# One table phase per sample on ScalarE in the first attention, with two full products ahead of each set of score tiles

## The reference, cut to what matters

```python
x = x + _L0_attn_a_ref(_layernorm(x), Wq, Wk, Wv, Wo)
x = x + _L0_ffn_ref(_layernorm(x), router_w, e_bias, Wg, Wu, Wd, SWg, SWu, SWd)
x = x + _L0_attn_b_ref(_layernorm(x), qkv_w, qkv_b, proj_w, proj_b)
x = x + _L0_ffn_ref(_layernorm(x), router_w, e_bias, Wg, Wu, Wd, SWg, SWu, SWd)

# _L0_attn_a_ref, 16 heads of 8 features
diff_sq = jnp.maximum(q_norm_sq + k_norm_sq - 2.0 * qk, 0.0)
denom = jnp.maximum((1.0 - q_norm_sq) * (1.0 - k_norm_sq), 1e-06)
cosh_arg = jnp.maximum(1.0 + 2.0 * diff_sq / denom, 1.0)
distance = jnp.where(cosh_arg > 1.0, jnp.arccosh(jnp.maximum(cosh_arg, 1.0 + 1e-12)), 0.0)
attn = jax.nn.softmax(-distance, axis=-1)

# _L0_ffn_ref routes each token: sigmoid scores, the best 4 of 8 groups by their two best
# experts, the best 8 experts in them, and their scores normalised are the coefficients
```

## Time and profile before

| | |
|---|---|
| time, median of 3 runs | 1120.06 us (1116.53 to 1122.86) |
| the profiled execution | 1117.54 us, its span 1115.8 us |
| PE, DVE, ACT, POOL busy | 88%, 88%, 62%, 32% of the span |
| mean granted TensorE clock | 0.86 of full speed |

### The profile page before, as it was taken

How to read it: one execution, slowest core, us unless ns; L and a number is a source line. 1 busy time by engine, 2 the same in 40 slices (tenths; PEclk the granted TensorE clock), 3 DMA queues, 4 the chain that set the end, 5 groups by cost and what they waited for, 6 DMA issues and landing times. The chain is left out here.

```text
span 1115.8 us, 17424 instructions
## 1 busy us (share of the span) xinstructions
PE 976.6 (88%) x5387; PEld 705.7 (63%) x5387; DVE 977.7 (88%) x1480; ACT 693.2 (62%) x791; POOL 359.8 (32%) x226
## 2 busy tenths in 40 slices
PE   7756766676768999999999899999879999999997
PEld 5533434343437788888888645455557888888886
DVE  7799888988978999999999787889688999999997
ACT  4789999999965445554455553666635445554454
POOL 2045655565450334333332120100112333433330
PEclk9855555555558999999999998999989999999999
DMA  2000000000104855555551000011228565555531
GB/s 57 1 1 1 1 1 1 0 1 0 36 15 119 207 153 151 151 147 158 153 151 46 1 1 1 10 20 17 44 69 211 155 156 151 149 150 153 156 86 38
DMA packets 50710, 86.93 MB, mean 78 GB/s; under 512 B 20092, under 2 KB 33404, under 8 KB 50556
## 3 DMA queue, kind: packets, MB, share of 16 engines
q1 hardware_dynamic: 50664, 86.34, 29.7%
HBM read 83.33 MB, written 2.98 MB: 77 GB/s over the span
## 5 line engine op out<-in xcount | busy, mean ns | idle before, releaser
L1450 ACT ACTIVATE sg<-ps 128x512 f32<-128x512 f32 x264 | 156.7, 594 | 265.7 <-PE ps L499 264.1
L499 PE MATMUL ps<-xh,whi 128*128 128x512 f32 x528 | 206.3, 391 | 1.3 <-ACT b L1274 1.3
L499 PE MATMUL ps<-xl,whi 128*128 128x512 f32 x528 | 205.9, 390 | 0.0
L499 PE MATMUL ps<-xh,wlo 128*128 128x512 f32 x528 | 205.8, 390 | 0.0
L2231 DVE TENSOR_TENSOR hf<-sg,ps 128x512 f32<-128x512 f32 x264 | 170.4, 684 | 30.8 <-DVE hl L2238 24.6
L1589 POOL TENSOR_TENSOR rr<-xr,rr 128x2048 f32<-128x2048 f32 x32 | 144.9, 4549 | 157.8 <-ACT xr L1253 94.9
L1649 POOL CAST whi<-wraw 128x384 fp32r<-128x384 f32 x66 | 66.5, 1008 | 367.2 <-PE ps L499 288.0
L2238 DVE TENSOR_TENSOR hl<-hf,hh 128x1024 fp32r<-128x1024 f32 x132 | 179.7, 1362 | 0.5 <-DVE hf L2231 0.5
L2243 DVE TENSOR_TENSOR hf<-hf,cbc 128x1024 f32<-128x1024 f32 x128 | 157.2, 1228 | 13.4
L1490 ACT ACTIVATE hh<-hf 128x1024 fp32r<-128x1024 f32 x132 | 139.2, 1055 | 4.3 <-DVE hf L2243 4.3
L1651 POOL TENSOR_TENSOR wlo<-wraw,whi 128x384 fp32r<-128x384 f32 x66 | 117.0, 1772 | 5.3
(11 more groups left out here) (276 smaller groups left out, 1580.3 us busy)
## 6 DMA issues: line engine op xcount, KB each, us to landing
cbc<-routing_coefficients SPq DMA_DIRECT2D x256, 256.0 KB, 3.8
wraw<-in_wexp_dram SPq DMA_DIRECT2D x66, 192.0 KB, 2.7
X<-in_x_dram SPq DMA_DIRECT2D x4, 256.0 KB, 4.5
routing_coefficients<-cT SPq DMA_DIRECT2D x8, 128.0 KB, 2.3
out_dram<-X SPq DMA_DIRECT2D x4, 256.0 KB, 2.9
heads_by_row<-o_all SPq DMA_DIRECT2D x12, 72.0 KB
b_rows<-heads_by_row SPq DMA_DIRECT2D x12, 72.0 KB, 2.7
rope_in<-in_consts_dram SPq DMA_DIRECT2D x1, 512.0 KB, 3.4
```

What stands on the lines that cost most here:

```text
L499: return pe.matmul(o, l, r, start=start, stop=stop, **kw)
L1450: act.activation(sg[c % 2][:, :], bank(4 + 2 * (c % 2)), ACT.Silu).then_inc(s_sg, 1)
```

## The change

ScalarE's step becomes a whole sample: the roots of its four chunks, one table load, its four logarithms and four exponentials, one table load. The first sample takes all roots in halves, without products; later the product form is used for the even chunks. TensorE's `pv_a` is cut in halves of four matmuls, put into slots by the table `PV_AT`; `diff` and `recip` each get `keep_busy(.., 2)` behind their wait and ahead of their tiles. The chain of the output of two samples ago moves two units earlier. VectorE's `product` stands behind units 3 and 5, the norms of groups 0 and 1 are taken in the last sample, and more of the first routing is done ahead of the last sample's output, for which the routing has a second set of tiles. In the end of the stage ScalarE makes sigmoid scores of the first half by exponentials, and table loads fall away. Line numbers on this side are those of the changed kernel.

```diff
 def diff(U):                                   # TensorE
     if U >= 1:
         pe.wait_ge(s_N, U)
+        keep_busy(0, 2)
...
 def recip(U):
     if U >= 1:
         pe.wait_ge(s_X, U)
+        keep_busy(2, 2)
...
+PV_AT = {5: (1, 0, 0), 6: (1, 0, 1), 8: (1, 1, 0), 9: (1, 1, 1),
+         11: (1, 2, 0), 12: (1, 2, 1), 15: (1, 3, 0), 0: (2, 3, 1)}
...
             diff(U + 1)
+        pv_step(s, 2 * u)
+        if U + 1 < B * UNITS:
             recip(U + 1)
-        if u % 2 == 0 and 4 * s - 5 + u // 2 >= 0:
-            C = 4 * s - 5 + u // 2
-            pv_a(C // CHUNKS, C % CHUNKS)
+        pv_step(s, 2 * u + 1)
         if 2 <= s:
-            if u == 3:
+            if u == 1:
                 o_token_major(s - 2)
+            elif u == 3:
+                o_transposed(s - 2)
             elif u == 5:
-                o_transposed(s - 2)
-            elif u == 7:
                 o_projected(s - 2)
...
 # ScalarE, samples_a
-    for half in range(1, 2 * B):
...
-        act.wait_ge(s_P, half)
-        act.activation(o, o, ACT.Sqrt).then_inc(s_R, 1)
...
-        act.preload_act_table_set("natural_log_exp_and_others")
-        if half == 1:
-            logs(1, 1.0, None, -2.0)
-        else:
-            logs(odd - 2, 2.0, one_c[:, 0:1], -1.0)
-        logs(even, 1.0, None, -2.0)
+    for s in range(B):
+        first = CHUNKS * s
+        for C in range(first, first + CHUNKS) if s >= 1 else ():
+            w, xw = rr[:, C % RR, :], xr[:, C % XR, :]
+            if by_product(C):
...
+                act.wait_ge(s_P, (C - CHUNKS) // 2 + 1)
+                act.activation(w, w, ACT.Sqrt).then_inc(s_R, 1)
+            else:
+                act.wait_ge(s_X, 2 * (C + 1))
...
+        act.preload_act_table_set("natural_log_exp_and_others")
+        log(first)
+        log(first + 1)
+        exp(first)
+        log(first + 2)
+        if s == B - 1:
+            f_norm_rstd(0, 2)
+            logit_exps(0, 0)
+        exp(first + 1)
+        log(first + 3)
+        exp(first + 2)
+        exp(first + 3)
...
 # VectorE, samples_a
+    if s == B - 1 and u in (0, 3):
+        dve.wait_ge(s_ores, 4)
+        norm_stats(0, u // 3, s_fstat)
     clamp(U)
...
     ratio(U)
-    if u % 4 == 3 and U > 3:
-        product(U // 2)
+    if s >= 1 and u in (3, 5):
+        product(CHUNKS * s + u - 3)
```

More of the change, by code:

```diff
@@ L64, in sync, with __init__, tile @@
         self.eng.wait_ge(self.sem, self.n)
+class RouteTiles:
+    def __init__(self, sb, f):
+        def tile(name, *shape):
+            return sb(f"{name}_{f}", [P, *shape])
+        self.sc = [tile(f"sc{g}", LT, E) for g in range(2)]
+        self.sfc = tile("sfc", LT, E)
+        self.by_group = self.sfc[:, :, :].rearrange("p t (k e) -> p (t k) e", e=8)
+        self.top = [tile(f"top{k}", LT * 8, w) for k, w in enumerate((4, 2, 1))]
+        self.second = [tile(f"second{k}", LT * 8, w) for k, w in enumerate((4, 2, 1))]
+        self.lesser = [tile(f"lesser{k}", LT * 8, w) for k, w in enumerate((2, 1))]
+        self.gs = tile("gs", LT, 12)
+        self.g8 = tile("g8", LT, 8)
+        self.gr = tile("gr", LT, 12)
+        self.gm = tile("gm", LT, 8)
+        self.mk = tile("mk", LT, E)
+        self.k8 = tile("k8", LT, 8)
+        self.mr = tile("mr", LT, E)
+        self.wsel = tile("wsel", LT, E)
+        self.wsum = tile("wsum", LT)
+        self.wrec = tile("wrec", LT)
+        self.coef = tile("coef", LT, E)
 def hybrid(nc, x, consts, wA, wB, bqk, brow, rwT, wexp, out):
@@ L215, in hybrid @@
                 sb("route_pad", [P, ROUTE_PAD])
[L216 to L231, removed]
+                route = [route_0, RouteTiles(sb, 1)]
         s_x = [sem(f"x_group_loaded{g}") for g in range(GROUPS)]
@@ L669, in pv, with pv_a, pv_step, o_token_major @@
                 return last
-            def pv_a(s, c):
+            PV_AT = {5: (1, 0, 0), 6: (1, 0, 1), 8: (1, 1, 0), 9: (1, 1, 1),
+                     11: (1, 2, 0), 12: (1, 2, 1), 15: (1, 3, 0), 0: (2, 3, 1)}
+            def pv_a(s, c, mt):
                 C = CHUNKS * s + c
[L673 to L681, removed]
+                if mt == 0:
+                    pe.wait_ge(s_W, C + 1)
+                    if c == 0 and s >= 1:
+                        pe.wait_ge(s_ev, s)
+                last = pv(vt, s, c, rr[:, C % RR, :], bank(4, 2)[:, c * N:(c + 1) * N], (mt,))
+                if mt == MT - 1:
+                    last.then_inc(s_pv, 1)
+            def pv_step(s, at):
+                if at in PV_AT:
+                    back, c, mt = PV_AT[at]
+                    if s >= back:
+                        pv_a(s - back, c, mt)
+            def o_token_major(s, half=None):
+                pe.wait_ge(s_ev, s + 1 if half != 1 else s + 2)
+                if s >= 1 and half != 1:
                     pe.wait_ge(s_ores, s)
                 for m in range(MT):
-                    for c in range(CHUNKS):
+                    for c in range(CHUNKS) if half is None else (2 * half, 2 * half + 1):
                         last = pe.transpose(bank(6 + m)[:, c * P:(c + 1) * P], osb[:, c, m * P:(m + 1) * P], ident)
-                last.then_inc(s_oP, 1)
+                if half != 0:
+                    last.then_inc(s_oP, 1)
             def o_transposed(s):
@@ L1407, in f_norm_std, with f_norm_apply_group @@
                 act.activation(std[g][:, :], mv[g][:, :, 1], ACT.Sqrt, bias=eps_s[:, 0:1]).then_inc(s_fstd, 1)
-            def f_norm_apply_group(f, g):
+            def f_norm_apply_group(f, g, tiles=range(GTILES)):
                 act.wait_ge(s_foff, GROUPS * f + g + 1)
-                for j in range(GTILES):
+                for j in tiles:
                     last = act.activation(f_xn[g][:, j, :], X[:, g * GTILES + j, :], ACT.Identity,
@@ L2034, in samples_a @@
                 norm_stats(0, 3, s_fstat)
+                route_coefs(0, 0)
                 f_offset(0, 3)
+                for j in range(2):
+                    last = dve.tensor_scalar(f_xn[3][:, j, :], X[:, 3 * GTILES + j, :], mv[3][:, j, 0:1],
+                                             rstd[3][:, j:j + 1], ALU.subtract, ALU.mult)
+                last.then_inc(s_fxh, 1)
             def prepare_b():
```

289 lines of the change are left out of this document (153 added, 136 removed).

## The result

The changed kernel takes 1167.88 us (median of four runs, 1165.68 to 1179.6), the kernel before, on the same chip, 1118.57 us: a ratio of 1.0457 with a 95% interval of 1.0379 to 1.0534. It is slower by 4.6%; 1110 us was forecast, with a range up to 1136. The profiled execution took 1165.68 us, 48.1 more than that of before.

The account below looks back on a forecast made before the run. ScalarE was taken to set the first attention's pace. 78.85 + 2 + 7 x 30.0 + 2.5 + 53 = 346.4 us to the expert loop, against 356.6, -10.2 us; 1120.1 - 10.2 = 1110 us, range 1099 to 1136.

Parts of the forecast that it names:

- Table loads: First attention, ScalarE: two of four loads a sample go, saving 2.57 us; its floor falls from 31.8 to 29.2 us.
- The step that failed: First attention: full products make four units a sample late at half clock, 2 us on top of VectorE's 27.9.
- a unit of 3.0 us: One unit at half clock: clamp 1.22, products 0.9, tiles 0.79, two handovers of 0.05, against 2.46 for two VectorE operations.
- my end of the range: First attention: TensorE's busy time at half clock, 22.4 + 32 x 0.45 = 36.8 us, as a sample's slow end.
- The forecast of 30.0 us: Length of a first-attention sample after the change, just over ScalarE's 29.2, with 29.2 and 36.8 us as ends.
- The clock: First attention: TensorE's clock rises in each sample and falls again at a product, mean 0.65 to 0.85.
- the two rests that I had named: TensorE's two pauses of 2 to 3 us a sample, behind units 3 and 5, while VectorE runs ratio, product and clamp.
- where I had put 2: First sample: eight units at half clock would lose 4 us, at full clock nothing; +2 us taken.
- the 5 us that the part behind it was to lose: Between ScalarE's last exponential and the expert loop: 5 us less, between 0 and 8, from routing work moved ahead.
- VectorE's need: First attention: busy time left at 27.9 us a sample, falling to some 27 if products lie where GpSimd rests.
- the value products' places: First attention, TensorE's queue: value products in halves are no new work; waits for their weights counted at nothing.
- The rival: First attention mostly at half clock, TensorE's 36.8 us set the sample: 1141 to 1161 us; decides above 31.5 us; chance 0.18.

Follow-up runs that it names:

- The loads put back: Changed kernel without its full products, with two more table loads in each sample between the second logarithm and the first exponential: 1125.32 us, ratio 1.0059.
- the run with the rests filled: Changed kernel with its full products, plus twelve products of 256 columns ahead of the waits of `diff(5)` and `diff(7)`: 1135.49 us, ratio 1.0155.
- the joined halves: Changed kernel with its full products, each chunk's value products in one piece at the place of the second half: 1137.73 us, ratio 1.0198.
- the run with the short product: Changed kernel with VectorE's second `product` of each sample computing only the first half of its columns: 1183.9 us, ratio 1.0581.
- products alone: Kernel before the change, with nothing but the two full products ahead of each set of tiles: 1153.06 us, ratio 1.0311.

## Why the prediction was wrong

- **Table loads: right.** ScalarE's need fell from 31.56 to 28.35 us (forecast: a floor of 29.2). The loads put back cost 2.72 us of it, 1.36 each, which is their 1.283 us and hardly more. The 5.3 us that the Trainium skill's page ScalarE: Activation LUTs, "What ACT_TABLE_LOAD costs", would give with its drain are ruled out here.
- **The step that failed: "the cost is then some four units of a sample at half clock, 4 x 0.5 = 2 us".** Its 0.5 us came from a unit of 3.0 us, in which I had put one pair of products. A unit has two sets, each with its own pair, and TensorE goes through them in sequence: 2 x (2 x 0.43 + 0.29 + 0.72) = 3.74 us. So a unit at half clock is 1.3 us late, not 0.5. Besides, the output chain and the value products come on top of the sets on TensorE, in whose time nothing was left. Four such units, the share at half clock that the forecast took, are 5.1 us, and 27.9 + 5.1 is a sample of 33.0. The row that measures all of it is 40.86 us a sample at half clock, where my end of the range was 36.8; the missing part is the change of kind, in no term of the sum: 22.4 + 32 x 0.43 + 16 x 0.29 = 40.8 us.
- **The forecast of 30.0 us contradicted its own ends.** A mean clock of 0.75 is half of the time at each level. With samples of 29.2 us at full clock and 36.8 at half, the rates of the two (samples per us) average to one of 32.6 us, and by the forecast's own sum 78.9 + 2 + 7 x 32.6 + 2.5 + 53 = 364.6 us, 8 us slower than before. Time lost at half clock isn't made up at full, since ScalarE's 28 us are the floor there. With the measured ends (28.0 and 40.9 us) the samples at 0.84, 0.70, 0.73, 0.62 and 0.58 should take 31.1, 34.5, 33.7, 36.8 and 38.1 us; they took 31.1, 35.2, 37.2, 39.7 and 41.6. What is over in the last three goes with VectorE's busy time (28.4 to 30.9 us, against 25.9 and 26.2 in the first two), most of which is its `product` stretched to 4.5 to 6.7 us.
- **The clock: right in kind.** It rose and fell, with 0.58 to 0.84 in the five samples; over the stage (60 to 345 us) the mean was 0.63, just under the 0.65 to 0.85 forecast. With products in the two rests that I had named it stayed up. The Trainium skill's page TensorE: Matmul & The Clock Gate, "A second HAM failure mode", lays such ups and downs to short idles between groups; the run with the rests filled agrees. Rests are not all of it: sample 0 was late by 9.8 us where I had put 2, since it stayed at half clock all through, though TensorE had no rest in it from 61 us on.
- **Where the 57.7 us between the forecast's 346.4 and the measured 404.14 are:** 7.8 in sample 0; 45.8 in the other seven, 36.9 us each with the two norms, against 30.4; 4.1 in the stretch to the expert loop. In that stretch the first part came as forecast (20.8 us from the last ratio to the last exponential, against 21.9), but the 5 us that the part behind it was to lose did not come: 36.3 us, against 36.2 before. Without products the whole stretch takes 66.8 us (274.91 to 341.71), not 53, so the forecast of that term was wrong there too; that the time of that kernel lies near my 1110 us is in part luck, samples of 28.0 us on average making up for it.
- **VectorE and the value products.** I had let VectorE's need fall to 27 us since its products would lie where GpSimd rests. They do without full products (2.60 us on average, in the kernel without them), but once VectorE is late the roots, and GpSimd's additions with them, start beside its second product. In the timeline above the product loses 4.4 us, one whole addition of 4.5 us, and not a part of both. The Trainium skill's page SBUF — State Buffer, "SBUF: two separate sides", says just that: VectorE with two inputs in SBUF and GpSimd hold their common ports by turns, for a whole instruction. That the joined halves gave 1138 us shows that the value products' places, which I had counted at nothing, matter too. That they do so by way of the clock fits its windows and is not shown.
- **The rival** that the products become the bound gave 1141 to 1161 us by the right mechanism, with the deciding point of 31.5 us a sample well passed, and still too little. "For it: the clock did not rise in 240 us in which PE was 70% busy" deserved more than 0.18. And the whole trade had little to win: at full clock a sample takes 28.0 to 28.1 us, at half clock without products 28.4.

Still open is what lets the clock rise. TensorE without any rest stayed at half clock for 151 us in the run with the short product. With the same products it rose from some 114 us on with joined halves, and with four products in each set, or at the first fill, it rose in the middle of unbroken work. Two of the kernels whose clock swings also repeat less well (1131 to 1149 us with joined halves, 1146 to 1159 with products alone, against 1114 to 1122 for the kernel before beside the latter). Which of two like kernels gets more of the full clock I could not have told beforehand, and can't now.

## What to carry to other kernels

Before work is added to raise a clock, ask what the stage would take at full clock: if another engine is the bound there, there is nothing to buy. Work put behind a wait, between the two engines that take turns, was paid by half to two thirds of its TensorE time at the lower clock here, even where it seemed covered, since all that stands behind it in the queue comes later too; only ahead of the wait, and no more than the rest holds, was it free. And when a stage swings between two rates with no catching up, its pace is the mean of the two paces weighted by the time at each, so work out both ends from whole samples, every matmul and every change of kind in it, before guessing where between them it lies.

## What the hardware showed that I had not expected

- Going from a full product to tiles of 32 rows costs 0.29 us at half clock, once in each set, beside the 0.43 us of each product; three sets of tiles in a row take 1.58 us, where two products and a set take 1.87.
- VectorE's `product` of 2.28 us took up to 6.7 us beside GpSimd's additions, as if it waited for a whole one, where 3.93 was the most before. It comes once VectorE is late, so a delay made on TensorE grows on VectorE: 41.6 us a sample with the stretch and 37.2 without it, at clocks of 0.58 and 0.59.
- A TensorE busy all the time (151.38 of 151.38 us) was granted half its clock; the same products with 24 more a sample in its two rests, busy 26.84 of 28.10 us, were granted all of it.
